# Which engine adds the masks and copies the turned probabilities in the first masked many-head attention stage

## What is computed

```python
def _L0_xattn_ref(q, k, v, attention_mask, Wq, bq, Wk, bk, Wv, bv):
    qh = (q @ Wq.T + bq).reshape(B, Sq, N_HEAD, D_HEAD)      # 16 heads of 16
    kh = (k @ Wk.T + bk).reshape(B, Sk, N_HEAD, D_HEAD)
    vh = (v @ Wv.T + bv).reshape(B, Sk, N_HEAD, D_HEAD)
    scores = jnp.einsum('bqhd,bkhd->bhqk', qh, kh) / np.sqrt(D_HEAD)
    scores = jnp.where(attention_mask[:, None, :, :], NEG_FILL, scores)
    probs = jax.nn.softmax(scores, axis=-1)
    out = jnp.einsum('bhqk,bkhd->bqhd', probs, vh)
    return out.reshape(B, Sq, N_HEAD * D_HEAD)
...
x = x + _L0_attn_ref(_layernorm(x, axis=-1), L0_attn_qk, L0_attn_ov)
x = x + _L0_xattn_ref(_layernorm(x, axis=-1), ctx_1024, ctx_1024, mask_BxSxS2_bf0, ...)
x = x + _L0_ffn_ref(...)
```

## Time and profile before

| | |
|---|---|
| median of three executions | 795.63 us |
| the profiled execution: its time, its span | 796.95 us, 795.1 us |
| busy in the span: TensorE matmul, VectorE, ScalarE, GpSimd | 96%, 66%, 53%, 42% |
| stage 1: first and last scores | about 67 us to 208 us |
| granted TensorE clock, 80 to 200 us | full speed throughout |

### The profile page before, as it was taken

One profiled execution on the slowest core, in us unless ns is written; L12 is line 12 of the kernel. 1 busy time (PEld: TensorE's weight loads), 2 busy tenths in 40 slices (PEclk: granted clock), 3 DMA queues, 4 the chain that ended last, 5 costly groups with the idle time before them and its releaser, 6 DMA issues.

```text
span 795.1 us, 16990 instructions
## 1 busy us (share of the span) xinstructions
PE 760.9 (96%) x6045; PEld 620.5 (78%) x6045; DVE 521.3 (66%) x1418; ACT 424.4 (53%) x1254; POOL 332.1 (42%) x457
## 2 busy tenths in 40 slices
PE   7999999999899999999999999999999999999997
PEld 6887777776788888877777777777777777888886
DVE  4575788787622343137767767777899887566656
ACT  2445677677532222337777766666665676423320
POOL 3134333443233212314222316666678745715550
PEclk9999999999999999999999999999999999999999
DMA  8902234322052226000000003000000001235538
GB/s 309 390 2 75 74 84 124 89 75 75 6 143 74 74 74 148 14 1 2 1 2 2 2 2 120 15 15 14 15 15 28 28 27 42 88 93 164 163 108 317
DMA packets 57569, 61.46 MB, mean 77 GB/s; under 512 B 21296, under 2 KB 48176, under 8 KB 56464
## 3 DMA queue, kind: packets, MB, share of 16 engines
q1 hardware_dynamic: 54080, 51.03, 20.8%
q0 software_dynamic: 3408, 9.34, 3.5%
HBM read 31.10 MB, written 29.27 MB: 76 GB/s over the span
## 4 chain that ended last, share of the span: by engine, by line
PE 66%; DVE 12%; POOL 7%; issue 6%; ACT 5%; DMA 2%; SPq 1%; POOLq 0%; DVEq 0%; ACTq 0%
PE pj L373 10%; PE pj L366 8%; PE pj L460 8%; PE ov L536 7%; PE sc L523 7%; PE sc L449 6%; POOL routed_y L1770 5%; DVE mx L1005 4%; PE ov L471 4%; PE pj L360 4%; ACT pr L1499 3%; PE sc L444 2%; PE sc L666 2%; PE ov L373 2%; PE pj L480 1%
## 5 line engine op out<-in xcount | busy, mean ns | idle before, releaser
L1499 ACT ACTIVATE pr<-sc,mx 128x128 f32<-128x128 f32 x768 | 215.8, 400 | 81.0 <-DVE mx L1005 79.4
L1005 DVE TENSOR_REDUCE mx<-sc 128x4 f32<-128x512 f32 x192 | 124.4, 683 | 37.1 <-PE sc L449 35.1
L460 PE MATMUL pj<-idn,pr 128*128 128x128 f32 x768 | 122.1, 284 | 6.3 <-ACT pr L1499 2.5
L460 PEld LDWEIGHTS pj<-idn,pr 128*128 128x128 f32 x768 | 86.4, 143 | 39.7 <-issue 20.7
L1012 DVE COPY pT<-pj 128x512 f32<-128x512 f32 x128 | 87.1, 686 | 32.9 <-PE pj L460 31.9
L1687 POOL TENSOR_SCALAR ve<-mv 128x2 f32<-128x2 f32 x40 | 14.1, 353 | 188.2 <-DVE mv L936 187.8
L1517 ACT ACTIVATE hT<-sc,vecs 128x256 f32<-128x256 f32 x64 | 30.4, 474 | 90.6 <-PE sc L523 90.6
L523 PE MATMUL sc<-xnT,W 128*128 128x256 f32 x256 | 64.1, 380 | 0.0
L536 PE MATMUL ov<-W,hT 128*128 128x256 f32 x256 | 60.5, 381 | 0.0
L449 PE MATMUL sc<-kM,qT 32*128 32x256 f32 x768 | 55.0, 399 | 4.4 <-ACT pr L1499 4.0
L1770 POOL DMA_INDIRECT routed_y<-pr,mask x39 | 37.5, 961 | 39.8 <-DVE pr L1253 39.8
(11 more groups left out here) (227 smaller groups left out, 1545.1 us busy)
## 6 DMA issues: line engine op xcount, KB each, us to landing
sorted_x<-more_xT SPq DMA_DIRECT2D x15, 1152.0 KB, 7.1
kM<-sorted_x SPq DMA_DIRECT2D x39, 129.0 KB, 2.1
cT<-in_ctxT SPq DMA_DIRECT2D x16, 256.0 KB, 3.4
W<-in_w SPq DMA_DIRECT2D x2, 1024.0 KB, 12.6
cT<-in_ctx SPq DMA_DIRECT2D x8, 256.0 KB, 3.0
W<-in_w_gu SPq DMA_DIRECT2D x1, 2048.0 KB, 8.2
hT<-routed_y SPq DMA_DIRECT2D x8, 256.0 KB, 5.6
out_x<-X SPq DMA_DIRECT2D x8, 256.0 KB, 3.9
```

What stands on the lines that cost most here:

```text
L460: last = tr(bank[b][:, i * S:(i + 1) * S], pr[n % 4][:, i, :], idn[:])
L1005: v.tensor_reduce(mx[n % 4][:], four(b), AX.X, ALU.max, negate=True).then_inc(mx_done, 1)
L1499: last = a(pr[n % 4][:, i, :], bank[b][:, i * S:(i + 1) * S], ACT.Exp, bias=mx[n % 4][:, i:i + 1])
```

## The change

Two tables of numbers get other entries for stage 1. Group 1 of the first half and group 5 of the second are now masked by VectorE and no longer by TensorE, and they are copied by ScalarE and no longer by VectorE. Stages 3 and 4 keep their entries. In the 16 halves this takes 16 mask matmuls from TensorE, gives 16 additions to VectorE and takes 16 copies from it, and gives 16 copies to ScalarE.

```diff
-        ACT_TURNS = {1: (2, 6), 3: (2, 6), 4: (1, 3, 5, 7)}
-        DVE_MASKED = {1: (2, 3, 6, 7), 3: (), 4: (3, 7)}
+        ACT_TURNS = {1: (1, 2, 5, 6), 3: (2, 6), 4: (1, 3, 5, 7)}
+        DVE_MASKED = {1: (1, 2, 3, 5, 6, 7), 3: (), 4: (3, 7)}
```

## The result

The changed kernel takes 815.48 us (median of four, 813.55 to 816.14), against 794.64 for the kernel before beside it. The ratio is 1.0263, with a 95% interval of 1.0242 to 1.0283: 20.9 us slower. The profiled execution took 816.14 us, 19.2 more than the profiled one of before. The forecast was 820, in a range of 810 to 834.

A forecast was written before the change was run, and what follows sets the result against it. Bound by a chain of waits alternating between TensorE and VectorE, with ScalarE without slack in the first half. 5 x 3.02 + 3 x 2.5 = 22.6 us gave a median of 818.2; one or two clock falls made 820, range 810 to 834.

The forecast's parts named there:

- What bounds: Attention stage: waits stay on TensorE in the first half, VectorE paces the second; ScalarE has no slack in the first.
- The cheap terms: 16 mask matmuls at 0.21 us save 3.4 us if TensorE bounds; VectorE's load unchanged; ScalarE's copy costs some 0.5 us.
- First half: Group 1's maxima wait behind three additions, delaying ScalarE's list; scores start at 149.04 instead of 147.79, 1.25 us lost.
- the step of one group of exponentials: ScalarE's list: start-to-start time of one group, taken as 1.11 us, half of 2.23.
- Second half: Group 5's copy follows late exponentials on ScalarE; `turn_x` starts 1.98 later, less one mask matmul 0.21: 1.77 us lost.
- The sum: Attention stage: five units at 3.02 us plus three at 2.5 give 22.6 us, 819.5 on the profiled execution, 818.2 as median.
- The clock: TensorE waiting more may fall to half clock; one fall priced at 1.2 us, one or two included, making 820 us.
- the stalls: Waits of TensorE in the attention stage from the new order on VectorE and ScalarE, 22.6 us in all.
- The rival that the clock falls in every unit: TensorE in the thin second half: 8 to 16 falls at 1.2 us, 828 to 837 us; falls in most units, chance 0.26.
- Half of the delay: ScalarE catches up or group 5's copy does not hold `turn_x`; one loss stays, 805 to 810 us; chance 0.11.
- TensorE's load: TensorE, busy 96%, sets every half; 16 mask matmuls are a pure 3.4 us gain, 792.2 us; chance of faster 0.04.

The follow-up runs named there:

- Nobody masks: Kernel before with the mask of groups 1 and 5 of stage 1 left out, no matmul and no addition: 0.9970 of its time (0.9953 to 0.9987).

## Why the prediction was right

*What bounds.* It read the chain as alternating between TensorE and VectorE, with ScalarE at its heels in the first half. "Nobody masks" confirms it: 0.21 us more room for TensorE gained nothing in a regular first half and all of it in the second.

*The cheap terms.* VectorE's busy time stayed (521.3 and 521.6 us). The mask matmul was priced right, and the 3.4 us that 16 of them could be worth are 2.2 in the stage when nothing takes their place.

*First half.* Predicted a loss of 1.25 us, measured 1.09. The path is the one named, instruction by instruction. The term that was mis-sized is the step of one group of exponentials. I took half of the 2.23 us that two groups filled, 1.11. Unhindered they follow each other at 1.02 (172.33 to 173.35) or 1.00 (174.30 to 175.30). The merged line of eight instructions had a wait for the maxima of group 1 inside it, which the view doesn't print. With two such steps the sum was too long by 0.2; the last group, 1.23 us instead of 1.15, takes some of it back.

*Second half.* Predicted 1.77, measured 1.60, in the main for the same reason (one such step, 0.1): from the start of group 5's exponentials to L360 I had 157.06 - 152.68 = 4.38 us, and it is 166.65 - 162.42 = 4.23.

*The sum.* 22.6 us were predicted, and the stage with what follows it shows 20.0 + 0.7. The five regular units gave 13.4 instead of 15.1. The other three parts gave 6.5 before the last half, as against 7.5 for the three units whole. Of the 4.5 us by which 820 is too high, this is 1.9; the clock, below, is 1.8, and 1.0 is the kernel before, which had a median of 794.64 beside the changed one and not 795.63. All three err to the same side, so the forecast owes nothing to errors that cancel.

*The clock.* I added 1.8 us for one or two falls on top of the stalls. The fall of the earlier trace rows is there again, in the stage's last half, and one more was seen ahead of it, in the first half of U = 15. TensorE had stood still for a whole microsecond there:

```profile
212.00:213.00 1.00, 0.00 (x0) 0.00 (x0) 1.00 (x3) 0.96 (x4) 0.00 (x0) 1.00 0.00 0
213.00:214.00 1.00, 0.68 (x4) 0.71 (x5) 0.93 (x5) 1.00 (x4) 0.00 (x0) 0.73 0.00 0
214.00:215.00 1.00, 1.00 (x7) 0.94 (x6) 0.34 (x1) 1.00 (x5) 0.00 (x0) 0.50 0.00 0
```

No run separates what this fall cost. That half grew by 1.8 us in all, and this is within the 20.7 above, so the 1.8 us that I added on top were not needed. The rival that the clock falls in every unit is out: from 80 to 200 us the clock was 1.00 with TensorE 83% busy. The Trainium skill (TensorE: Matmul & The Clock Gate, Part 4) says that a transpose does not count as busy time in the way another matmul does. The trace shows no fall from that: from 161.94 to 167.14 TensorE ran nothing but turns, with waits of 1.11, 0.33 and 0.79 us between them (I had expected 1.3, 0.5 and 1.3), and the clock stayed at full speed.

*The other rivals.* Half of the delay: no, both halves lost. TensorE's load: no, by "nobody masks".

The prediction's sum has both parts of the change in one chain and never prices them apart. The runs add that in the second half they cost 0.60 and 0.44 alone and 1.60 together. They also show a second path that the sum for this half leaves out, since the copy of group 5 ends later: VectorE's values, late by the third addition. With both places in the order repaired, this path keeps 0.43 us of the loss.

## What to carry to other kernels

Where each engine works through a list in order, find what is queued behind a moved operation, on its engine and then on the next, and what slack each has. Its place in the list decided most of the cost here: the same work in another order was worth 2.2 us of 19.9 a unit in the changed kernel, and cost 0.7 of 17.2 in the kernel before. Its length counted where its engine was itself on the path: once the order was mended, the third addition's 0.60 us showed in the second half. Balanced busy times say nothing about either. And when an edit is good in the steady state, look at the units at the stage's ends, where lists of two stages mix and a later copy can stop TensorE long enough for its clock to fall.

## What the runs showed of the hardware

On VectorE an addition to a 128x512 PSUM tile and a maximum of another one start 0.60 us apart, but 0.80 apart when the maximum reads what the addition wrote (150.97 to 151.77). A group of four exponentials of 128x128 takes ScalarE 1.00 to 1.02 us from its start to that of the next instruction when nothing holds them (174.30 to 175.30, 172.33 to 173.35). A fall of TensorE's clock to half stretched the scores from 1.15 to 2.09 us and four transposes (L360) from 0.65 to 1.04, 1.5 us in all; it came after a stretch in which TensorE was busy 0.01 and 0.32 us of two microseconds.
